# Spreading the narrow expert tiles, with the last weight pieces on TensorE and a new order of the routing tables: an adaLN block with spectral binding and a mixture of experts, one core of a Trainium2

## The reference

```python
h = layernorm(x) * (1 + ca) + sa                       # ca, sa, ... from c by one matmul
q, k, v = unit_projection(h @ Wq.T + bq), ...          # fft(x)/|fft(x)|, back to time
x = x + ga * unbind(cumsum(bind(k, v), axis=1), q)     # products of spectra, running sum over tokens
h = layernorm(x) * (1 + cb) + sb
weights, sel = top_k(h @ gate_w, 2); weights = softmax(weights)
y = swiglu(h @ dense_1[e].T + b1[e]) @ dense_2[e].T + b2[e]     # for the two experts e of each token
x = x + gb * sum_k weights_k * y_k                     # 8 experts, 512 hidden units each
```

## Time and profile before

| | us |
|---|---|
| median of 3 runs (595.48 to 599.93) | 595.83 |
| profiled execution, its own time | 594.5 |
| profiled execution, span from first to last instruction | 592.5 |
| TensorE busy (matmuls) | 548.7 (93%) |
| VectorE busy | 478.2 (81%) |
| GpSimd busy | 294.8 (50%) |
| ScalarE busy | 294.4 (50%) |

### The profile page before, as it was taken

One profiled execution on the slowest core, in us unless ns is written; L12 is line 12 of the kernel. 1 busy time (PEld: TensorE's weight loads), 2 busy tenths in 40 slices (PEclk: granted clock), 3 DMA queues, 4 the chain that ended last, 5 costly groups with the idle time before them and its releaser, 6 DMA issues.

```text
span 592.5 us, 13011 instructions
## 1 busy us (share of the span) xinstructions
PE 548.7 (93%) x3955; PEld 407.6 (69%) x3956; DVE 478.2 (81%) x1059; ACT 294.4 (50%) x497; POOL 294.8 (50%) x197
## 2 busy tenths in 40 slices
PE   8998999999999995667999999999999999999992
PEld 6545565555646552526588888888888888888771
DVE  1288979999999989999488888888888888888762
ACT  4776678879696863641533333333333333333330
POOL 0004033432423242000548888888888888887532
PEclk9998989999897977866999999999999999999998
DMA  8333633653745437723567787777777777765722
GB/s 310 121 99 122 184 97 109 191 160 107 212 107 153 125 97 246 289 42 70 144 118 137 143 134 136 131 138 129 139 134 135 141 129 133 130 98 86 113 38 28
DMA packets 81571, 79.32 MB, mean 134 GB/s; under 512 B 44596, under 2 KB 71348, under 8 KB 81272
## 3 DMA queue, kind: packets, MB, share of 16 engines
q0 software_dynamic: 16912, 31.74, 30.2%
q1 hardware_dynamic: 63320, 46.15, 27.5%
q10 hardware_dynamic: 1296, 0.87, 0.5%
HBM read 44.06 MB, written 22.23 MB: 112 GB/s over the span
## 4 chain that ended last, share of the span: by engine, by line
PE 73%; DVE 17%; ACT 3%; issue 3%; DMA 2%; POOL 1%; POOLq 0%; DVEq 0%; ACTq 0%
PE ps L778 31%; PE ps L799 15%; PE ps L530 11%; PE ps L589 4%; DVE region L1258 2%; PE ps L543 2%; PE ps L629 2%; PE ps L625 1%; DMA region<-in_dft 1%; PE ps L600 1%; PE ps L461 1%; PE ps L590 1%; DVE region L1273 1%; DVE region L1380 1%; DMA out_rows<-w_stage,region 1%
## 5 line engine op out<-in xcount | busy, mean ns | idle before, releaser
L778 PE MATMUL ps<-region,w_sb 128*128 128x256 f16 (+1 forms) x1872 | 200.4, 264 | 1.9 <-ACT region L1026 1.3
L778 PEld LDWEIGHTS ps<-region,w_sb 128*128 x1872 | 172.6, 98 | 24.9 <-issue 3.2
L1690 POOL DMA_INDIRECT out_rows<-w_stage,region x71 | 135.7, 1912 | 49.6 <-issue 20.0
L1680 POOL DMA_INDIRECT region<-h_scratch,region x71 | 95.9, 1351 | 71.5 <-DVE region L1539 45.0
L1571 DVE TENSOR_SCALAR region<-ps,region 128x256 f32<-128x256 f32 (+1 forms) x156 | 64.3, 454 | 55.3 <-PE ps L778 53.8
L799 PE MATMUL ps<-region 128*128 x852 | 99.5, 273 | 3.5 <-DVE region L1585 3.3
L1130 ACT ACTIVATE region<-ps,region 128x256 f32<-128x256 f32 (+1 forms) x156 | 62.2, 451 | 79.2 <-PE ps L778 74.2
L1142 ACT ACTIVATE region<-region 128x1024 f16<-128x1024 f32 (+1 forms) x39 | 38.2, 981 | 109.4 <-DVE region L1579 106.8
L799 PEld LDWEIGHTS ps<-region 128*128 128x128 f16 x852 | 82.6, 98 | 14.4 <-issue 4.3
L530 PE MATMUL ps<-region 128*128 128x512 f32 x192 | 84.2, 595 | 3.2 <-ACT region L894 3.2
L1660 POOL TENSOR_TENSOR region<-region 128x512 f32<-128x512 f32 x30 | 37.3, 1270 | 96.2 <-DVE region L1285 96.2
(11 more groups left out here) (229 smaller groups left out, 699.2 us busy)
## 6 DMA issues: line engine op xcount, KB each, us to landing
w_stage<-in_w SPq DMA_DIRECT2D x20, 512.0 KB, 3.8
region<-in_x SPq DMA_DIRECT2D x8, 512.0 KB, 7.5
out_rows<-region SPq DMA_DIRECT2D x8, 512.0 KB, 3.0
h_scratch<-gb_bc SPq DMA_DIRECT2D x4, 1024.0 KB, 6.7
h_scratch<-region SPq DMA_DIRECT2D x8, 512.0 KB, 3.2
region<-region POOLq DMA_DIRECT2D x7, 512.0 KB, 4.6
region<-in_ramp SPq DMA_DIRECT2D x1, 2064.0 KB, 10.6
region<-in_w SPq DMA_DIRECT2D x4, 512.0 KB, 6.0
```

What stands on the lines that cost most here:

```text
L778: mm = pe.matmul(ps[:, GV + 2 * half + a, (f % 2) * MT:(f % 2) * MT + wide], w, xg_t[:, s, xa * KD + k, 0:wide], start=(n == 0), stop=(n = ...
L1680: G.indirect_dma_start(out=xg_rows[:, t % XG, u, :], out_offset=None, in_=h_scratch, in_offset=bass.IndirectOffsetOnAxis(ap=gather_idx[:, ...
L1690: G.indirect_dma_start(out=out, out_offset=bass.IndirectOffsetOnAxis(ap=scatter_idx[:, at:at + 1], axis=0), in_=y_sb[:, t % 2, u, :], in_o ...
```

## The change

**Tiles.** The seven narrow tiles are now t = 0, 6, 12, 18, 24, 37 and 38 (`NARROW`); the others are wide. Slot columns keep their meaning: the wide tiles' columns come first (64), then the narrow ones' (7), so `col_of`, and the counts of `y_ready`, `scattered` and `xgt`, are computed for the new order. The hardware loop now runs for n = 1 to 3 and the last 15 tiles are written out. In every six, the last up part (m = 5) is the narrow one of the next six. VectorE does `low(t + 1)` ahead of `rows_out(t)` where tile t + 2 is narrow (m = 4 in the loop), and also for t = 37. Before the last `down` stand 8 `keep_warm` matmuls.

**Weights.** Two of the pieces of `low_weights(9)` are made before `rank_totals`, the other two and all of `low_weights(10)` between `rank_all` and `place_pairs`. `low_weights(11)`, the low halves of weights 22 and 23, is made by TensorE and ScalarE behind `place_pairs`; VectorE's two instructions for them are gone.

**Tables.** VectorE makes four columns of indices first (`near_idx`, for tiles 0 and 1), then the experts of the tiles and `te_word`, then all 71 columns of gather indices, then `scatter_idx`. TensorE and ScalarE wait for `tiles_ready` 2, the words, instead of 4; GpSimd's gathers from tile 2 on wait for 3. The 8 `keep_warm` matmuls before `first_rows(0)` are gone; 3 behind it stay.

Cut to what the text speaks of:

```diff
+NARROW = (0, 6, 12, 18, 24, 37, 38)
+FEW = NARROW.index(37)
+LOOPS = FEW - 1
+EVEN, ODD = 2 * SUB + 1, 3 * SUB
+AROUND = EVEN + ODD
+SO_FAR = [0] + [1 + SUB * m for m in range(XG)]
...
-    return SUB if t < BIG else 1
+    return 1 if t in NARROW else SUB
+
+
+def rows_to(t):
+
+    return sum(subs(i) for i in range(t))
 
 
 def col_of(t):
 
-    return SUB * min(t, BIG) + max(t - BIG, 0)
+    return SUB * BIG + NARROW.index(t) if t in NARROW else rows_to(t) - sum(n < t for n in NARROW)
...
-            def low_weights(t):
-
-                for i in range(4):
+            def low_weights(t, pieces=range(4)):
+
+                for i in pieces:
                     n, at = 2 * t + i // 2, (i % 2) * BLK
                     pe.wait_ge(w_hi, n + 1)
                     if i >= 2:
                         pe.wait_ge(w_lo[0], 2 * t + i - 1)
+                    else:
+                        pe.wait_ge(w_lo[1], 2 * t + i - 1)
...
+            low_weights(9, (0, 1))
             rank_totals()
             rank_all()
-            low_weights(9)
+            low_weights(9, (2, 3))
+            low_weights(10)
             place_pairs()
-            pe.wait_ge(w_lo[1], 2 * 10)
-            low_weights(10)
+            low_weights(11)
...
-                pe.wait_ge(gathered[t], 16 * SUB)
-                bank = ps[:, 3 - t, :].bitcast(FP16)
-                for u in range(SUB):
+                pe.wait_ge(gathered[t], 16 * subs(t))
+                if t == 1:
+                    pe.wait_ge(w_lo[1], W_CHUNKS)
+                bank = ps[:, 3 - 2 * t, :].bitcast(FP16)
+                for u in range(subs(t)):
...
+                    t, k = XG * n + m, m + 1
+                    arrived = EVEN * n + min(k // 2 * SUB, EVEN) if k % 2 == 0 else ODD * n + k // 2 * SUB
+                    up(t + 1, k % 2, e[k], None if first and m == 0 else 16 * arrived, wide=MT if k < XG else P)
+                    down(t, m % 2, e[m], None if first and m < 2 else AROUND * n + (SO_FAR[m - 1] if m else -SUB),
+                         parts=SUB if m else 1)
+
+            pe.wait_ge(tiles_ready, 2)
             e = experts(0)
-            keep_warm(8, ident_h[:], w1_sb[:, HI, 0:BLK], GV + 1)
             first_rows(0)
             keep_warm(3, ident_h[:], w1_sb[:, HI, 0:BLK], GV + 1)
-            up(0, 0, e[0], None, between=lambda: first_rows(1))
+            up(0, 0, e[0], None, between=lambda: first_rows(1), wide=P)
             for i in range(2):
                 pe.wait_ge(w_lo[i], W_CHUNKS)
             six_turns(0, first=True)
-            with pe.Fori(1, ROUNDS) as n:
+            with pe.Fori(1, LOOPS) as n:
                 six_turns(n)
-            for t in range(XG * ROUNDS, MOE_TILES):
+            for t in range(XG * LOOPS, MOE_TILES):
                 if t % XG == 0:
                     e = experts(t // XG)
                 if t + 1 < MOE_TILES:
                     up(t + 1, (t + 1) % 2, e[t % XG + 1], moved(t + 1, 2, 2), wide=P * subs(t + 1))
-                down(t, t % 2, e[t % XG], parts=subs(t))
+                if t == MOE_TILES - 1:
+                    keep_warm(8, ident_h[:], w1_sb[:, HI, 0:BLK], TP)
+                down(t, t % 2, e[t % XG], rows_to(t - 1), parts=subs(t))
...
+            near = [P, 2 * PARTS, SUB]
+
+            done(V.scalar_tensor_tensor(out=near_at, in0=halves, scalar=1.0,
+                                        in1=near_part.unsqueeze(2).to_broadcast(near), op0=ALU.is_ge,
+                                        op1=ALU.mult),
+                 V.tensor_scalar(near_k, halves, float(P * PC // TOP_K + 1), None, ALU.is_ge))
+            done(V.tensor_tensor(near_at, near_at, halves, ALU.add),
+                 V.tensor_reduce(near_second, near_k.rearrange("p (q h) i -> p (h i) q", q=PARTS), AX_X, ALU.add))
+            done(V.tensor_reduce(near_perm, near_at.rearrange("p (q h) i -> p (h i) q", q=PARTS), AX_X, ALU.add))
+            done(V.scalar_tensor_tensor(out=near_perm, in0=near_second, scalar=-float(P * PC // TOP_K), in1=near_perm,
+                                        op0=ALU.mult, op1=ALU.add))
+            V.tensor_scalar(near_idx, near_perm, -1.0, 0.0, ALU.add, ALU.max).then_inc(tiles_ready, 1)
...
+            done(V.tensor_reduce(odd_e, odd_at, AX_X, ALU.add),
+                 V.tensor_scalar(rounds[:, 0:ROUNDS, 1:XG], loop_e, float(EXPERTS - 1), None, ALU.min),
+                 V.tensor_scalar(tile_e[:, XG * ROUNDS:NARROW[FEW]], wide_e[:, (XG - 1) * ROUNDS:],
+                                 float(EXPERTS - 1), None, ALU.min),
+                 V.scalar_tensor_tensor(out=few_e, in0=few_e, scalar=float(EXPERTS), in1=few_e, op0=ALU.is_lt,
+                                        op1=ALU.mult))
+            done(V.tensor_tensor(rounds[:, 0:ROUNDS, 0], few_e[:, 0:FEW], odd_e[:, 0:FEW], ALU.add),
+                 V.tensor_tensor(tile_e[:, NARROW[FEW]:MOE_TILES], few_e[:, FEW:], odd_e[:, FEW:], ALU.add))
...
+            V.scalar_tensor_tensor(out=te_word, in0=rounds[:, 1:SIX + 2, 0], scalar=float(8 ** XG), in1=words,
                                    op0=ALU.mult, op1=ALU.add).then_inc(tiles_ready, 1)
+            spots = quarters[:, :, 0:SLOT_COLS]
...
-            for n in (22, 23):
-                dve.wait_ge(w_hi, n + 1)
-                hi, lo = parts_of(n)
-                V.scalar_tensor_tensor(out=lo, in0=staged(n), scalar=SW, in1=hi,
-                                       op0=ALU.mult, op1=ALU.subtract).then_inc(w_lo[n % 2], 2)
...
+                    t, s, wide = XG * n + m, m % 2, MT if m + 1 < XG else P
+                    hidden(t + 1, 1 - s, e[m + 1], wide=wide)
+                    if m == XG - 2:
+                        low(t + 1, 1 - s, wide=wide)
...
+                ahead_of = t + 1 < MOE_TILES and t + 2 in NARROW + (MOE_TILES,)
+                if ahead_of:
+                    low(t + 1, (t + 1) % 2, wide=P * subs(t + 1))
+                rows_out(t, t % 2, t % XG, e[t % XG], moved(t - 2, 2), col_of(t), rows_to(t), parts=subs(t))
+                if t + 1 < MOE_TILES and not ahead_of:
...
+                idx = near_idx[:, SUB * (1 - t) + u:SUB * (1 - t) + u + 1] if t < 2 else gather_idx[:, at:at + 1]
...
-                    pool.wait_ge(tiles_ready, 2)
+                    pool.wait_ge(tiles_ready, 3)
```

131 lines of the change are left out of this document (63 added, 68 removed).

## The result

Over 19 runs each, the changed kernel has a median of 594.77 us (591.89 to 595.92) and the kernel before one of 597.25 us (593.98 to 601.1). The ratio is 0.9948, with a 95% interval of 0.9927 to 0.997: about 3 us, half a per cent, faster. The forecast was 594.7 us.

The account below looks back on a forecast made before the run. TensorE was taken as the bound, without idle time from 304 to 540 us and waiting outside it. First up matmul to end -0.3, step into tile 0 -2.5, ranks +1.7: -1.1 us from 595.83, giving 594.7 us; range 589 to 600.

Parts of the forecast that it names:

- The ranks, +1.7 us: Two pieces ahead of the totals delay the totals, ranks and place_pairs by 1.7 us; bounds 0 and 2.2 us.
- The step into tile 0, -2.5 us: Before tile 0's first up matmul: warm matmuls gone -1.9 us, fewer transposes and smaller copy -0.7, tile word +0.1.
- rival 1: Busier TensorE holds 2.4 GHz: four pieces before tile 0 take 4.3 us, ranks lose nothing; 590.2 us, chance 0.18.
- The first tiles, 10.2 us: First up matmul to first down matmul: 10.2 us, against 11.5 us before.
- The transposes of tile 2, "6.6 us instead of 8.2 us", priced at nothing: Tile 2's transposes, issued when tile 0's up part ends, have 6.6 us to land instead of 8.2; no cost added.
- rival 3: Transposes behind narrow tiles land too late for 8.1 us: 2.4 us at each of five tiles, 606.7 us; chance 0.05.
- Narrow tiles, 0.15 us at each low half: Down part of the wide tile ahead of a narrow one waits 0.15 us for its low half; five places, 0.75 us.
- 0.2 us at each of four tile words, 0.8 us in all: At round starts, TensorE's jump and word load show 0.2 us at four places; bounds 0 and 5.2 us in all.
- Rival 2: Sequencer bounds every narrow tile, 5.7 us instead of 4.15, and word loads show 1.3 us each: 606.9 us; chance 0.09.
- The end, 25.85 us from the end of tile 37's up part: Last tiles: scatters each wait for the landing before, so 25.85 us follow tile 37's up part.
- rival 4: Last scatters don't queue for landings; 21.5 us follow tile 37's up part, 4.4 us less: 590.3 us, chance 0.12.
- From first up matmul to end, -0.3 us: First up matmul to end of span: 302.4 us before, 302.1 after; narrow tiles' gain mostly given back at the end.

Follow-up runs that it names:

- e1_behind: Changed kernel with the two low weight pieces ahead of the ranks put back behind them; 592.65 us, ratio 0.9965 to the kernel before.
- e2_warm: Changed kernel with the eight warm matmuls ahead of tile 0's transposes put back; 593.49 us, ratio 0.9984 to the kernel before.
- e5_word: Changed kernel with TensorE loading the tile word once, not again ahead of tile 1's up part; 595.06 us, ratio 0.9981 to the kernel before.
- e3_low: Changed kernel with the low half always behind the rows-out of the tile before; 595.38 us, ratio 0.9994 to the kernel before.
- e6b_hold: Changed kernel with the gathers of tiles 4 and 5 held until tile 2's transposes landed; 592.16 us, ratio 0.9927 to the kernel before.
- e4_front: Kernel before with only the part of the change ahead of the tiles, tile order and tables untouched; 594.6 us, ratio 0.9985 to the kernel before.
- e9_nowarm: Kernel of e6b_hold without the eight warm matmuls ahead of the last down part; 592.52 us in one run.
- e12_rows: Changed kernel, gathers of tiles 4 and 5 held, two low weight pieces moved, tile 35's rows-out ahead of tile 36's low half; 591.25 us, ratio 0.9915.
- e7_six: Kernel of e6b_hold with tile 30 narrow instead of tile 37; 595.16 us, ratio 0.996 to the kernel before.
- e11_moved_six: Kernel of e7_six with two of the last four low weight pieces moved to TensorE's waits; 593.56 us, ratio 0.9941 to the kernel before.

## Why the prediction was right, and where it was not

The forecast of 594.7 us and the median of 594.77 us agree better than the reasons do. The prediction gave the change 1.1 us; the ratio gives it 3.1 us (1.8 to 4.4), and the median of the kernel before is 1.4 us higher over its 19 runs than over the three that the forecast started from. The forecast gain was too small by about 1.4 us (1.1 against 2.5 us by the medians) and the starting point too low by 1.4 us: that the two cancel is luck. The stretches of the traces give 2.3 us for the 1.1 forecast.

- **The ranks, +1.7 us: right in place and size** (1.64 us to the totals, 1.7 us to the end of place_pairs). Whether another place is cheaper the prediction did not ask: in e1_behind's trace it was not. The prediction saw the one-hot rows as the cover of six pieces that end near 269. They ended at 274.3, where 2.23 us are this execution's lateness; of the other 3 us, two pieces ran at 1.2 GHz (2.2 us more) and one waited 0.62 us for ScalarE's table load, which the prediction had not looked for. What saved the 1.7 is that TensorE takes 1.94 us a group where VectorE takes 2.58: it was 1.6 us late with the first group and catches up 1.9 us in three.
- **The step into tile 0, -2.5 us: it was -3.5 us** (B). The four pieces took 6.2 us, not 7.1 (7.2 before): in this execution the clock rose earlier, at the second piece and not at the third. That is a small part of rival 1, and the executions show B between 7.2 and 8.3 us for this code. Rival 1 counts "ten pieces instead of eight" for itself. By the program there are twelve instead of eight, and eight instead of four ahead of place_pairs; even so the clock was at 1.2 GHz again when the pieces behind place_pairs began. The warm matmuls' share was 1.2 us and not 1.9 (e2_warm).
- **The first tiles, 10.2 us: 10.6 us.** That the load of the tile word "may show 0.1 us" missed the second load ahead of tile 1; most of 0.99 us was that (e5_word). Tile 0's own matmuls and transposes took 4.4 us where 4.95 were allowed.
- **The transposes of tile 2, "6.6 us instead of 8.2 us", priced at nothing: wrong.** This is the step of the prediction that failed. It took its bound for a landing from a quiet stretch (3.8 us) and priced a late landing only behind the narrow tiles of the loop (rival 3, which did not occur there). At tile 2, GpSimd starts three or four more gathers while the transposes run, and they took 7.7 to 11.2 us where TensorE had to wait (in e2_warm it did not). It cost 0.7 us in the profiled execution, 5 us in e3_low's, and e6b_hold removed it.
- **Narrow tiles, 0.15 us at each low half: right** (0.1 to 0.2). **0.2 us at each of four tile words, 0.8 us in all: too high**, 0.4 us once and nothing at the other three. Rival 2 did not occur; the up parts ran in 2.84 to 2.93 us. The Trainium skill's rule on a taken branch that has to wait for its fetch ("Runtime: NRT & Kernel Launch", Instruction fetch mechanics) would show as idle time at the rounds; the trace has none there beyond that 0.4 us.
- **The end, 25.85 us from the end of tile 37's up part: 24.2 us, but that up part took 3.41 and not 2.84 us**, (3.50 us from start to start), so 1.0 us less in all. The mechanism is right from tile 36's scatters on: landings set the end, and rival 4 did not occur. VectorE brought tile 36's rows to their scatters 1.1 us earlier than laid out, a landing is 4.5 us, not 4.7, and 5.8 us follow the last scatter, not 6.05. The trace has one wait that nobody named: tile 38's rows-out waits 1.70 us for the scatter of tile 36, whose buffer it needs (581.48). It lies behind the same chain of landings.
- **From first up matmul to end, -0.3 us: -0.6 us.** e4_front fits this: the order of the tiles gives little by itself (0.6 to 1.0 us).

## What to carry to other kernels

When work is put ahead of a wait, ask what it would cost in the other places too: in the one trace of it, eight pieces behind the ranks cost as much as six there and two ahead of them. A transfer that was hidden by a margin of 1 us must be priced with the traffic beside it, at the place where it runs; holding the gathers of two tiles that nobody needed yet gave 0.9 us in C, about what the new order of 39 tiles gave (0.6 to 1.0). And where each of several ordered transfers waits for the landing of the one before, the end of the kernel is counted in landings: move the work that feeds the first of them.

## What was not expected of the hardware

- A wait of 2.6 or 3.5 us in the middle of a stretch at 2.4 GHz was followed by 1.2 GHz, and the up part behind took 1.5 to 1.7 us longer (e1_behind 7.08, e3_low 6.92, else 5.41 us). So was the wait of 3.12 us in e9_nowarm. Waits of 0.7 to 1.4 us had no such effect (0.99 us ahead of tile 1's up part, then 5.41 us; 1.36 us in e12_rows, then 1.1 us for a piece), nor had one of 2.20 us ahead of the last down part of the kernel before (582.12, then 1.48 us).
- Which piece is the first at 2.4 GHz differs between executions of the same program, and moves stretch A by up to 0.9 us and most of B's 1.1 us. In the part ahead of it, which no edit touches, the same shows on a larger scale: the last gate matmuls start at 254.2 to 258.1 us.
- In three runs TensorE has "issue" idle between the matmuls of one up part, where no wait stands in the program: 0.15 us in e7_six, 0.95 us in e9_nowarm, 1.7 us in e11_moved_six, all in the second half of tile 0's up part, and others up to 0.5 us later. These three ran on one chip and the other experiments on three others, where none shows it. So C of these three is not to be set against that of the others, and only their stretch from tile 37's up part on is. No experiment was made on it, and its cause is open.
